# Attention masks of a decoder layer moved to GpSimd and made by saturating arithmetic, with constant operands on ScalarE

## The chip, the core and the metric

The kernel runs on one core of a Trainium2 chip. The core has five engines that run side by side, each with its own queue of instructions: TensorE (PE, matmuls), VectorE (DVE), ScalarE (ACT), GpSimd (POOL) and SyncE (SP), which here issues all DMAs. They wait for each other by semaphores. The metric is the device time of one execution in microseconds.

## What is computed

The kernel is one pre-norm decoder layer over x of shape (8, 128, 128): attention with a hyperbolic distance in 16 heads of 8, then a gated linear attention (mLSTM) over a context in 4 heads, then a mixture of 8 experts. The change is in the first part only:

```python
def _hyperbolic_attention(q, k, v, c, beta, causal=True):
    qn = jnp.sum(q * q, axis=-1)
    kn = jnp.sum(k * k, axis=-1)
    qk = jnp.einsum('bhnd,bhmd->bhnm', q, k)
    diff_sq = jnp.maximum(qn[..., :, None] - 2.0 * qk + kn[..., None, :], 0.0)
    ed = jnp.sqrt(diff_sq + EPS)
    ns = qn[..., :, None] + kn[..., None, :]
    dist_taylor = ed * (1.0 + c * ns * 0.5 + c * c * ns * ns * 0.125)
    dist_asymp = 0.693 + jnp.log(ed + EPS) + c * ns * 0.25
    dist_standard = ed * jnp.sqrt(1.0 + c * ns)
    dist = jnp.where(ed < 0.1, dist_taylor, jnp.where(ed > 2.0, dist_asymp, dist_standard))
    scores = -beta * dist
    if causal:
        scores = jnp.where(tril, scores, -jnp.inf)
    return softmax(scores) @ v
```

Each pair of a query and a key picks one of three formulas for its distance. The kernel works with squares: `e2` is diff_sq, and the two choices are the masks `m_ge` (e2 + 1e-8 >= 0.01, not the Taylor form) and `m_gt` (e2 > 4 - 1e-8, the logarithmic form).

## The kernel before

The attention is cut into 16 units. A unit is a batch and half of its heads, and because of the causal mask only three quarters of the score columns are computed: 768 columns over 128 partitions, in tiles of 128x768. The units pass through a software pipeline written out by hand: every engine has a function `step(s)`, and in step s it works on several units at different stages. All engines run the steps from -1 to 20 in order. Work of units below 0 or above 15 is left out, some steps are in hardware loops, and the last steps have parts of the next stage mixed in (`after`). Nothing reorders instructions within an engine: what is written first is issued first, and waits on semaphores hold everything that is queued behind them on that engine.

One unit u goes this way, with the step in which each engine does it:

- PE: scores P1 (for e2, step u-2) and P2 (for c times ns, `n1` in DVE's code, step u-1), from stacks that SP loads from DRAM. A stack serves two units of a pair of batches; the loads are issued ahead of need, when the scores of the previous holders are done.
- ACT, step u-1: `e2` (Relu, L676), `l1` (Ln of e2, L681), `sqn` (Square, L695) and `wt` (Square, L704), the last two for the Taylor factor.
- DVE, step u-1: `m_ge` (L969), after the wait for e2.
- POOL, step u-1: `m_gt` (L540). It is queued behind the causal additions of unit u-2.
- DVE, step u: `da` (L927, the logarithmic form), then wt is replaced by n1 where m_ge says so (L932, COPY_PREDICATED), then `prod` = (e2 + eps) * wt (L948, SCALAR_TENSOR_TENSOR with both tensors in SBUF).
- ACT, step u: `lp` (Ln of prod, L700) and `dist` (Exp of half of it, L713).
- DVE, step u+1, as the last instruction of the step: dist is replaced by da where m_gt says so (L984, COPY_PREDICATED).
- POOL, step u+1: the causal mask, an addition of 1e30 above the diagonal (L531 and L532, for each of two halves of the unit: four instructions).
- DVE, step u+2: row minima (L941, L943), and their split in three bf16 parts `nmp` (L958 CAST, L973, L976 CAST, L978). PE transposes these, ACT copies them as `shift` (L709), and PE transposes dist with the shift added, 12 pairs of matmuls.
- ACT, step u+3: `pT` (Exp, L686). PE, step u+3: the product with the values. DVE and ACT close a batch in every second pair of steps (L920, L935, L952, L964 and L690).

Tiles named e2, l1, wt, da and prod share one tensor and appear as `dist_mem` in the rows. `P` stands for the PSUM tiles P1, P2 and P3. `cf` is the table of constants: where an ACTIVATE has cf among its inputs, its bias or scale comes as a column of it, read from SBUF. m_ge, m_gt, e2 and da have two buffers each, dist has four. The line numbers in the rows are those of this kernel; matmuls all have L1183, that of a helper.

POOL also clears three tiles after step 5 (L553 to L555), and later splits the expert weights in two parts (L579, L582).

## Time and profile before

| | |
|---|---|
| median of 3 runs | 305.19 us (305.09 to 305.37) |
| span of the profiled execution | 302.1 us |
| PE busy | 224.5 us, 74% |
| DVE busy | 228.1 us, 76% |
| ACT busy | 171.9 us, 57% |
| POOL busy | 109.2 us, 36% |

The span is that of one profiled execution, from its first to its last instruction. The median time also holds what lies around the span. Attention fills the time from about 34 to 150 us; projections and loads stand ahead of it, and the second attention and the experts behind it. A timeline row gives start, duration, engine, line, operation, output<-inputs and shape, and in brackets how long the engine had been idle before it and what it had waited for.

### The profile page before, as it was taken

To read this page: it belongs to the slowest core of one execution; us is meant where nothing else is said; L and a number is where in the kernel's file an instruction comes from. 1 tells how busy PE (TensorE), PEld (TensorE's weight loads), DVE (VectorE), ACT (ScalarE), POOL (GpSimd) and SP (SyncE) were. 2 spreads that over 40 slices of the span, in tenths; PEclk is the share of its full clock that TensorE was granted. 3 is DMA by queue.
4 is the path that set the end of the run, shared out by engine and by line. 5 is a ranking of instruction groups with operands and counts; after the bars stand their busy time and mean duration, and the time that the engine had idled before them with its cause. 6 is when DMAs were issued, how large, how long until landed. Compare 5 with 4: busy or idle time off the path is not lost.

```text
span 302.1 us, 5293 instructions
## 1 busy us (share of the span) xinstructions
PE 224.5 (74%) x1624; PEld 179.0 (59%) x1624; DVE 228.1 (76%) x576; ACT 171.9 (57%) x291; POOL 109.2 (36%) x140
## 2 busy tenths in 40 slices
PE   0867233994778986577766990599896799999994
PEld 0434232773666766465344670487685698888984
DVE  6777799999989999997395349378669976746554
ACT  3599799999499999756511355233432136322320
POOL 5233326777755666652360000000234043424400
PEclk9997655556595579555855796599799599999999
DMA  6208879899404210000000000000000000010001
GB/s 161 69 13 201 171 190 223 195 351 218 116 1 96 48 45 20 0 22 0 1 2 0 0 0 0 2 1 1 2 0 0 0 2 1 2 35 0 0 0 35
DMA packets 38084, 16.80 MB, mean 56 GB/s; under 512 B 19240, under 2 KB 36016, under 8 KB 38064
## 3 DMA queue, kind: packets, MB, share of 16 engines
q1 hardware_dynamic: 38064, 16.56, 21.9%
q8 instruction: 10, 0.16, 0.2%
q14 instruction: 10, 0.08, 0.1%
HBM read 10.39 MB, written 4.98 MB: 51 GB/s over the span
## 4 chain that ended last, share of the span: by engine, by line
PE 44%; DVE 25%; SPq 13%; issue 9%; DMA 4%; ACT 2%; POOL 1%; DVEq 0%; ACTq 0%
PE P L1183 32%; PE PM L1183 7%; PE PO L1183 5%; SPq L369 4%; DVE dist L984 3%; SPq L434 2%; DVE dist_mem L932 2%; SPq L373 2%; DVE m_ge L969 1%; DVE nm L943 1%; DMA n_split<-nsl 1%; SPq L378 1%; DVE dist_mem L948 1%; DMA k_split<-split_mem 1%; SPq L479 1%
## 5 line engine op out<-in xcount | busy, mean ns | idle before, releaser
L782 ACT ACTIVATE dist_mem<-P,gub 128x512 f32<-128x512 f32 x32 | 21.9, 688 | 53.1 <-PE P L1183 51.5
L579 POOL CAST whi<-wgu 128x512 fp32r (+1 forms) x16 | 9.9, 617 | 101.8 <-PE P L1183 101.8
L1112 DVE SCALAR_TENSOR_TENSOR dist_mem<-P,gub,dist_mem 128x512 f32<-128x512 f32 x32 | 23.7, 749 | 22.8 <-ACT dist_mem L782 22.7
L540 POOL TENSOR_SCALAR m_gt<-dist_mem 128x768 uint8<-128x768 f32 x16 | 34.3, 2144 | 6.7 <-issue 4.4
L1183 PE MATMUL P<-cf,dist 128*128 128x128 f32 x96 | 30.0, 398 | 6.6 <-ACT shift L709 6.6
L1183 PE MATMUL P<-xhi,whi 128*128 128x512 f32 x64 | 28.7, 448 | 4.6 <-DVE dist_mem L1112 4.0
L531 POOL TENSOR_TENSOR dist<-dist,cf 128x128 f32<-128x128 f32 x32 | 14.6, 458 | 47.5 <-DVE dist L984 47.5
L1183 PEld LDWEIGHTS P<-cf,dist 128*128 128x128 f32 x96 | 19.5, 203 | 13.4 <-ACT shift L709 9.3
L1183 PE MATMUL P<-shift,cb 128*128 128x128 bf16 x96 | 27.4, 294 | 0.0
L1183 PE MATMUL P<-xlo,whi 128*128 128x512 f32 x64 | 27.2, 425 | 0.0
L1183 PE MATMUL P<-xhi,wlo 128*128 128x512 f32 x64 | 27.2, 425 | 0.0
L1183 PE MATMUL PO<-v_st,pT 128*64 128x9 f32 (+1 forms) x384 | 24.8, 238 | 3.2 <-ACT pT L686 3.1
L1183 PEld LDWEIGHTS PO<-v_st,pT 128*64 128x64 f32 x384 | 23.0, 181 | 5.7 <-ACT pT L686 3.9
L1183 PE MATMUL P<-stn,stq 128*128 128x128 bf16 (+1 forms) x128 | 12.3, 265 | 15.7 <-DVE dist_mem L932 15.7
L582 POOL TENSOR_TENSOR wlo<-wgu,whi 128x512 fp32r<-128x512 f32 x16 | 20.4, 1278 | 2.9 <-POOL whi L579 2.9
L1183 PEld LDWEIGHTS P<-stn,stq 128*128 128x128 bf16 x128 | 9.6, 128 | 19.4 <-issue 19.3
L1183 PE MATMUL P<-stk,stq 128*128 128x128 bf16 (+1 forms) x128 | 11.8, 258 | 8.6 <-DMA stn<-n_split 8.2
L1183 PEld LDWEIGHTS P<-xhi,whi 128*128 128x128 f32 x64 | 13.2, 206 | 7.6 <-issue 5.0
L984 DVE COPY_PREDICATED dist<-m_gt,dist_mem 128x768 f32<-128x768 uint8 x16 | 16.4, 1024 | 0.9
L932 DVE COPY_PREDICATED dist_mem<-m_ge,P 128x768 f32<-128x768 uint8 x16 | 16.3, 1016 | 0.9 <-ACT dist_mem L704 0.9
L927 DVE SCALAR_TENSOR_TENSOR dist_mem<-dist_mem,P 128x768 f32<-128x768 f32 x16 | 15.2, 950 | 2.2 <-ACT sqn L695 1.4
L686 ACT ACTIVATE pT<-P,nbeta 128x768 f32<-128x768 f32 x16 | 14.2, 888 | 3.9 <-PE P L1183 3.8
(221 smaller groups left out, 603.4 us busy)
## 6 DMA issues: line engine op xcount, KB each, us to landing
q_split<-split_mem SPq DMA_DIRECT2D x16, 128.0 KB, 2.8
k_split<-split_mem SPq DMA_DIRECT2D x4, 512.0 KB, 3.6
stq<-q_split SPq DMA_DIRECT2D x16, 128.0 KB
stk<-k_split SPq DMA_DIRECT2D x16, 128.0 KB
v_st<-vab SPq DMA_DIRECT2D x8, 144.0 KB, 2.4
wgu<-gate_w SPq DMA_DIRECT2D x1, 1024.0 KB, 8.7
wgu<-up_w SPq DMA_DIRECT2D x1, 1024.0 KB, 11.3
x_sb<-x SPq DMA_DIRECT2D x2, 256.0 KB, 3.0
```

Of the source, the lines that this page charges most:

```text
L369: sp.dma_start(sq_[k][half[j], :, j, :], q).then_inc(stack_in[k], 16)
L531: pool.tensor_tensor(wideq, wideq, cm, ALU.add)
L540: pool.tensor_scalar(m_gt[:, g.k % 2, :], e2[:, g.k % 2, :], 4.0 - ATT_EPS, None, ALU.is_gt).then_inc(sm["gt_done"], 1)
L579: pool.tensor_copy(hi, w).then_inc(sm["whi_done"], 1)
L582: pool.tensor_tensor(lo, w, hi, ALU.subtract).then_inc(sm["w_ready"], 1)
L686: A(row(pT, t.k % 2), P3[:, :, 0:384], ACT.Exp, scale=nbeta[:, :]).then_inc(sm["pT_done"], 1)
L782: A(sil[:, f, :], P[:, 0, :], ACT.Silu, bias=gub[:, 0, bass.ds(e * FC + f, 1)]).then_inc(sm["sil_done"], 1)
L927: V.scalar_tensor_tensor(row(da, p), row(l1, p), 2.0, n1, ALU.mult, ALU.add).then_inc(sm["da_done"], 1)
L932: V.copy_predicated(row(wt, p), row(m_ge, p), n1).then_inc(sm["sel_done"], 1)
L984: V.copy_predicated(dist[:, far.k % 4, :], m_gt[:, far.k % 2, :], da[:, far.k % 2, :]).then_inc(sm["dist_done"], 1)
L1112: V.scalar_tensor_tensor(hT[:, 2 * slot + f, :], (P1, P2)[f][:, 1, :], gub[:, 1, bass.ds(e * FC + f, 1)], sil[:, f, :], ALU.add, ALU.mult) ...
L1183: return nc.tensor.matmul(out_, lhsT, rhs, start=start, stop=stop, **more)
```

## The change

`m_ge` moves from DVE to POOL, where it is queued between the causal additions and m_gt, with the waits it had (e2_done and sel_done). Both masks are made by addition and multiplication instead of a comparison: e2 minus the limit, times 2 to the 40th, written to uint8. Negative values become 0 and positive ones 255, and a predicated copy takes everything but 0 as true. The limit of m_ge is the largest number that still gives the reference's choice (`below`). The four causal additions become two of twice the size. On ACT four column operands of three instructions (l1's bias, sqn's scale and bias, wt's bias) are constants in the instruction instead.

```diff
+def below(limit, eps):
+    limit, eps = np.float32(limit), np.float32(eps)
+    e = limit
+    while np.float32(e + eps) >= limit:
+        e = np.nextafter(e, np.float32(0))
+    return float(e)
+NEAR_TOP = below(0.01, ATT_EPS)
...
                     wait(pool, "dist_done", g.n(1))
-                    for i in range(2):
-                        row = dist[:, g.k % 4, i * 384:(i + 1) * 384]
...
-                        pool.tensor_tensor(wideq, wideq, cm, ALU.add)
-                        last = pool.tensor_tensor(near, near, cm, ALU.add)
-                    last.then_inc(sm["causal_done"], 1)
+                    rows = dist[:, g.k % 4, :].rearrange("p (i n) -> p i n", i=2)
...
+                    pool.tensor_tensor(wideq, wideq, cm, ALU.add)
+                    pool.tensor_tensor(near, near, cm, ALU.add).then_inc(sm["causal_done"], 1)
                 g = s + 1
                 if g.there():
                     wait(pool, "e2_done", g.n(1))
+                    wait(pool, "sel_done", g.n(-1))
+                    pass_waits(pool)
+                    pool.tensor_scalar(m_ge[:, g.k % 2, :], e2[:, g.k % 2, :], -NEAR_TOP, 2.0 ** 40, ALU.add,
+                                       ALU.mult).then_inc(sm["ge_done"], 1)
                     wait(pool, "dist_done", g.n(-1))
                     pass_waits(pool)
-                    pool.tensor_scalar(m_gt[:, g.k % 2, :], e2[:, g.k % 2, :], 4.0 - ATT_EPS, None,
-                                       ALU.is_gt).then_inc(sm["gt_done"], 1)
+                    pool.tensor_scalar(m_gt[:, g.k % 2, :], e2[:, g.k % 2, :], ATT_EPS - 4.0, 2.0 ** 40, ALU.add,
+                                       ALU.mult).then_inc(sm["gt_done"], 1)
...
-                    A(l1[:, p, :], e2[:, p, :], ACT.Ln, scale=LN_SHIFT, bias=col(K_SEPS)).then_inc(sm["l1_done"], 1)
+                    A(l1[:, p, :], e2[:, p, :], ACT.Ln, scale=LN_SHIFT, bias=LN_SHIFT * ATT_EPS).then_inc(sm["l1_done"], 1)
...
-                    A(row(sqn), ps2, ACT.Square, scale=col(K_R8), bias=col(K_R8)).then_inc(sm["sqn_done"], 1)
+                    A(row(sqn), ps2, ACT.Square, scale=8 ** -0.5, bias=8 ** -0.5).then_inc(sm["sqn_done"], 1)
...
-                    A(wt[:, p, :], sqn[:, :], ACT.Square, bias=col(K_HALF)).then_inc(sm["wt_done"], 1)
+                    A(wt[:, p, :], sqn[:, :], ACT.Square, bias=0.5).then_inc(sm["wt_done"], 1)
...
-                if near.there():
-                    wait(dve, "e2_done", near.n(1))
-                    wait(dve, "sel_done", near.n(-1))
-                    V.tensor_scalar(m_ge[:, near.k % 2, :], e2[:, near.k % 2, :], ATT_EPS, 0.01, ALU.add,
-                                    ALU.is_ge).then_inc(sm["ge_done"], 1)
```

On POOL, one step in the hardware loop stands like this before; dist is the tile with the causal mask added, dist_mem is e2, and the names in brackets are the semaphores waited for:

```order
L531 TENSOR_TENSOR dist<-dist,cf 128x2x64 [waits dist_done]
L532 TENSOR_TENSOR dist<-dist,cf 128x128
L531 TENSOR_TENSOR dist<-dist,cf 128x2x64
L532 TENSOR_TENSOR dist<-dist,cf 128x128
L318 REGISTER_ALU
L540 TENSOR_SCALAR m_gt<-dist_mem 128x768 [waits e2_done,dist_done]
```

and like this now:

```order
L542 TENSOR_TENSOR dist<-dist,cf 128x2x2x64 [waits dist_done]
L543 TENSOR_TENSOR dist<-dist,cf 128x2x128
L330 REGISTER_ALU
L550 TENSOR_SCALAR m_ge<-dist_mem 128x768 [waits e2_done,sel_done]
L554 TENSOR_SCALAR m_gt<-dist_mem 128x768 [waits dist_done]
```

The additions are two instead of four, and m_ge has come in ahead of m_gt.

On DVE, a step of the fill of the pipeline from dist to the split of the minima stands like this before:

```order
L984 COPY_PREDICATED dist<-m_gt,dist_mem 128x768 [waits da_done,ds_done,gt_done]
L927 SCALAR_TENSOR_TENSOR dist_mem<-dist_mem,P 128x768 [waits dist_done,sqn_done,l1_done]
L932 COPY_PREDICATED dist_mem<-m_ge,P 128x768 [waits ge_done,wt_done]
L941 TENSOR_REDUCE nm<-dist 128x2x2 [waits causal_done]
L943 TENSOR_REDUCE nm<-dist 128x2x2
L948 SCALAR_TENSOR_TENSOR dist_mem<-dist_mem 128x768 [waits lp_done,sel_done]
L958 CAST nmp<-nm 128x8 [waits nmT_full,nm0_done]
L969 TENSOR_SCALAR m_ge<-dist_mem 128x768 [waits sel_done,e2_done]
L973 TENSOR_TENSOR nmr<-nm,nmp 128x8 [waits nm1_done]
```

and like this now:

```order
L993 COPY_PREDICATED dist<-m_gt,dist_mem 128x768 [waits da_done,ds_done,gt_done]
L941 SCALAR_TENSOR_TENSOR dist_mem<-dist_mem,P 128x768 [waits dist_done,sqn_done,l1_done]
L946 COPY_PREDICATED dist_mem<-m_ge,P 128x768 [waits ge_done,wt_done]
L955 TENSOR_REDUCE nm<-dist 128x2x2 [waits causal_done]
L957 TENSOR_REDUCE nm<-dist 128x2x2
L962 SCALAR_TENSOR_TENSOR dist_mem<-dist_mem 128x768 [waits lp_done,sel_done]
L972 CAST nmp<-nm 128x8 [waits nmT_full,nm0_done]
L982 TENSOR_TENSOR nmr<-nm,nmp 128x8 [waits nm1_done]
```

The instruction that made m_ge is gone between the cast and the subtraction, and with it its waits; the rest keeps its order.

## Rows read from the trace of the kernel before

**Rows 1.** The page's strip of 40 slices of 7.55 us, busy tenths.

```profile
DVE  6777799999989999997395349378669976746554
ACT  3599799999499999756511355233432136322320
PEclk9997655556595579555855796599799599999999
```

**Rows 2.** Timeline of PE: unit 8's scores.

```profile
76.77 0.80 PE L1183 MATMUL P<-stk,stq 128*128 128x128 bf16 x8 [3.88 <-DMA stn<-n_split]
```

**Rows 3.** Timeline of DVE, one step between two instructions of L984.

```profile
91.67 1.03 DVE L984 COPY_PREDICATED dist<-m_gt,dist_mem 128x768 f32<-128x768 uint8 x1
...
94.52 0.68 DVE L941 TENSOR_REDUCE nm<-dist 128x4 f32<-128x512 f32 x1
...
95.44 0.95 DVE L948 SCALAR_TENSOR_TENSOR dist_mem<-dist_mem 128x768 f32<-128x768 f32 x1
...
96.38 0.73 DVE L969 TENSOR_SCALAR m_ge<-dist_mem 128x768 uint8<-128x768 f32 x1
97.04 0.15 DVE L973 TENSOR_TENSOR nmr<-nm,nmp 128x8 f32<-128x8 f32 x1
97.22 0.17 DVE L976 CAST nmp<-nmr 128x8 bf16<-128x8 f32 x1
...
97.66 1.02 DVE L984 COPY_PREDICATED dist<-m_gt,dist_mem 128x768 f32<-128x768 uint8 x1
```

**Rows 4.** Timeline of POOL in the same step.

```profile
92.78 0.46 POOL L531 TENSOR_TENSOR dist<-dist,cf 128x128 f32<-128x128 f32 x1 [2.18 <-DVE dist L984]
...
94.03 0.46 POOL L532 TENSOR_TENSOR dist<-dist,cf 128x128 f32<-128x128 f32 x1
94.57 2.13 POOL L540 TENSOR_SCALAR m_gt<-dist_mem 128x768 uint8<-128x768 f32 x1
```

**Rows 5.** Groups of DVE from 79 to 135 us: count, busy us, mean ns.

```profile
L969 DVE TENSOR_SCALAR m_ge<-dist_mem 128x768 uint8<-128x768 f32 x8 | 4.7, 589 | 0.0
```

**Rows 6.** Groups of POOL by shape, whole span.

```profile
L540 POOL TENSOR_SCALAR m_gt<-dist_mem 128x768 uint8<-128x768 f32 x16 | 34.3, 2144 | 6.7 <-issue 4.4 <-ACT dist_mem L676 1.1
L582 POOL TENSOR_TENSOR wlo<-wgu,whi 128x512 fp32r<-128x512 f32 x16 | 20.4, 1278 | 2.9 <-POOL whi L579 2.9
L531 POOL TENSOR_TENSOR dist<-dist,cf 128x128 f32<-128x128 f32 x32 | 14.6, 458 | 47.5 <-DVE dist L984 47.5
...
L579 POOL CAST whi<-wgu 128x512 fp32r x14 | 8.6, 614 | 101.8 <-PE P L1183 101.8
...
L567 POOL COPY ctx<-ctx_sb 128x1024 f32<-128x1024 f32 x1 | 1.0, 1036 | 0.0
```

**Rows 7.** Line 948 over the whole span: duration min/median/max in ns.

```profile
L948 DVE SCALAR_TENSOR_TENSOR dist_mem<-dist_mem x16: 942/950/1350, 38.6 to 137.5; 128x768 f32<-128x768 f32 x16
```

**Rows 8.** Timelines of POOL and DVE where line 948 was longest.

```profile
38.34 2.13 POOL L540 TENSOR_SCALAR m_gt<-dist_mem 128x768 uint8<-128x768 f32 x1 [1.12 <-ACT dist_mem L676]
...
38.62 1.35 DVE L948 SCALAR_TENSOR_TENSOR dist_mem<-dist_mem 128x768 f32<-128x768 f32 x1
```

**Rows 9.** Timeline of DVE while POOL clears tiles.

```profile
74.66 3.01 DVE L976 CAST nmp<-nmr 128x8 bf16<-128x8 f32 x1
```

**Rows 10.** Timeline of DVE in the drain.

```profile
149.81 0.69 DVE L941 TENSOR_REDUCE nm<-dist 128x4 f32<-128x512 f32 x1 [1.80 <-POOL dist L532]
```

**Rows 11.** Groups of ACT from 79 to 126 us.

```profile
L713 ACT ACTIVATE dist<-lp 128x768 f32<-128x768 f32 x8 | 6.6, 827 | 0.0
L681 ACT ACTIVATE dist_mem<-dist_mem,cf 128x768 f32<-128x768 f32 x7 | 6.6, 937 | 0.2
```

**Rows 12.** Timeline of PE: the first transposes of two steps.

```profile
98.72 0.48 PE L1183 MATMUL P<-cf,dist 128*128 128x128 f32 x1 [0.36 <-ACT shift L709]
...
104.70 0.48 PE L1183 MATMUL P<-cf,dist 128*128 128x128 f32 x1 [0.36 <-ACT shift L709]
```

**Rows 13.** A stretch of 2 us: busy PE, PEld, DVE, ACT, POOL; PEclk, DMA share, GB/s.

```profile
102.00:104.00 2.00, 2.00 (x28) 1.86 (x26) 1.87 (x8) 2.00 (x3) 0.67 (x1) 0.50 0.39 62
```

More of the change, by code:

```diff
@@ L525, in step @@
                     wait(pool, "dist_done", g.n(1))
-                    for i in range(2):
-                        row = dist[:, g.k % 4, i * 384:(i + 1) * 384]
-                        wideq = row[:, 0:256].rearrange("p (j n) -> p j n", j=2)[:, :, HALF:128]
-                        near = row[:, 256:384].rearrange("p (j n) -> p j n", j=2)
-                        cm = cf[:, C_CM:C_CM + HALF].unsqueeze(1).broadcast_to([128, 2, HALF])
-                        pool.tensor_tensor(wideq, wideq, cm, ALU.add)
-                        last = pool.tensor_tensor(near, near, cm, ALU.add)
-                    last.then_inc(sm["causal_done"], 1)
+                    rows = dist[:, g.k % 4, :].rearrange("p (i n) -> p i n", i=2)
+                    wideq = rows[:, :, 0:256].rearrange("p i (j n) -> p i j n", j=2)[:, :, :, HALF:128]
+                    near = rows[:, :, 256:384].rearrange("p i (j n) -> p i j n", j=2)
+                    cm = cf[:, C_CM:C_CM + HALF].unsqueeze(1).unsqueeze(1).broadcast_to([128, 2, 2, HALF])
+                    pool.tensor_tensor(wideq, wideq, cm, ALU.add)
+                    pool.tensor_tensor(near, near, cm, ALU.add).then_inc(sm["causal_done"], 1)
                 g = s + 1
@@ L910, in step @@
                 n1 = P2[:, :, 0:384]
-                low, far, near = s - 2, s - 1, s + 1
+                low, far = s - 2, s - 1
                 t = s - 4
```

## The prediction

> **What bounds the kernel now.** I read the strip of the span in 40 slices first. VectorE (DVE) is busy 9 tenths or more in slices 6 to 18, with one at 8, and ScalarE (ACT) nearly as much, so in the attention pipeline both look full, and TensorE (PE) runs there mostly at the lower of its two levels [rows 1]. The change touches only this pipeline, roughly 34 to 150 us, and what it shortens must be looked for there; the expert layers behind it have other bounds.
>
> Next I ask where the pipeline is pinned from outside. At 76.77 the score matmuls of unit 8 had waited 3.88 us for the DMA that brings their operands [rows 2]. SyncE's queue before it holds weights and stores and is not waiting for attention work at that point, so whatever the first eight units (0 to 7) gain only lengthens this wait. The gain has to come from units 8 to 15, after 77 us, and from the drain.
>
> There one step of the pipeline takes about 6 us, and the timeline of DVE through one step shows no idle time: `COPY_PREDICATED` into dist at 91.67, and the next one at 97.66, 5.99 us later, with all work laid end to end between [rows 3]. GpSimd (POOL) works 3.9 us of that step and waits 2.18 us for DVE's dist [rows 4]. ACT has next to no idle time either, but the chain of waits of this stretch runs along DVE's instructions. So DVE is what sets the pace, with ACT and, in some steps, PE just under it.
>
> **m_ge leaves DVE.** Eight instructions of line 969 lie behind 77 us, 589 ns on average [rows 5]. The next instruction starts some 0.08 us before such a one ends, so they hold DVE for 4.7 - 8 x 0.08 = 4.1 us. The part of this that is already waiting is included: at 96.38 the instruction took 0.73 us where it takes 0.55 alone, because POOL's m_gt ran until 96.70 [rows 3, 4]. All of it is on the path, as DVE has no gap. Upper end of the gain here: 4.1 us.
>
> **What POOL's instructions cost.** Two facts are needed, and the trace shows neither directly: the price of an add-and-multiply over 768 columns into uint8, and of an addition of 256 columns.
> The additions: 128 columns take 458 ns, 512 columns 1278 ns, both with two inputs [rows 6], so 2.14 ns a column; 256 columns come to 0.73 us, and two of them take 1.4 us where four take 1.7 us. Saved on POOL: 0.3 us a step.
> The masks: the comparison takes 2144 ns for 768 columns, 2.8 ns each. Instructions with one input that don't compare take 614 ns for 512 columns and 1036 ns for 1024, 0.82 ns a column, which gives 0.83 us for 768 [rows 6]. These are the two ends: 0.83 us, if the comparison is what is dear in m_gt, and 2.14 us, if it is the kind of instruction or the uint8 output. I take 0.83 us: the new form is arithmetic on one input, and reading can't be what holds m_gt up, as its input seems to be read within 0.68 us (next part). I keep 2.14 for the rivals.
> The Trainium skill (GPSIMD Engine Reference, section 4.1) says that one-input elementwise work on GpSimd runs at roughly line rate. The row of m_gt speaks against it as a rule for all such work; by the rule the new masks cost what I take, and the row of m_gt taken for the price of every mask leads to the 318 us of the last rival.
>
> **What POOL's instructions do to DVE.** They share a way into SBUF, and this is where the change can pay back its gain. Three things are seen. A `CAST` on DVE that met POOL's memsets took 3.01 us instead of 0.17, through several of them without getting in between [rows 9, 3]. A DVE instruction with two SBUF inputs, line 948, took 1350 ns when it started 0.28 us after an m_gt, 0.40 more than its median of 950 [rows 7, 8]; so m_gt held the reading side until 0.68 us after its start. The same instruction met every later m_gt about 0.9 us after its start and was not held: 15 of 16 are near 950 [rows 7, 3, 4].
> Now lay the new work of a step from the first causal addition at c = 92.78 [rows 4]. The two additions end at c + 1.42, m_ge starts at c + 1.50 (the gap before m_gt in the rows is 0.08), m_gt at about c + 2.38, and ends at c + 3.21. It reads until c + 3.06. Line 948 comes at 95.44, c + 2.66 [rows 3]: it is now held 0.40 us. The small `CAST` comes at c + 3.5 + 0.4, when POOL is done. So such a step gains 0.66 (m_ge with its wait, 96.38 to 97.04) - 0.40 = 0.26 us. In steps that also close a batch, a copy and a reciprocal stand before line 948, 0.2 us, and it is held 0.2 to 0.35 against 0.47 gained. I take 0.2 us a step for the seven steps from unit 8 to unit 14, 1.4 us, and 0.46 in full for the step at 80 to 86 us, where POOL's masks are over before line 948 runs. Together 1.9 us.
> The Trainium skill (SBUF — State Buffer, section Who interferes with whom) says that whoever comes first holds the shared port for its whole instruction. The 15 undisturbed rows of line 948 speak against this for reading. By that rule line 948 would be held until c + 3.21, 0.15 us longer, and the sum would be about 1 us smaller, 304.0.
>
> **The causal additions.** In the steady steps they end before DVE asks for them (94.49 against 94.52), so nothing is gained. In the drain DVE waits for them, 1.80 us up to 149.81, and there the chain passes through them [rows 10]: 0.3 us.
>
> **ScalarE's constants.** An `ACTIVATE` takes 827 ns with constants (L713) and 937 with one column operand (L681) [rows 11]. So a column costs about 0.1 us, and the change drops four a step, 0.40 us. ACT is hidden under DVE in these steps; what it buys is that ACT, which fills the step of 6 us as well, does not become the bound when DVE shrinks. Alone I value it at nothing; without it most of the 1.9 us would be stopped by ACT.
>
> **PE at its lower level.** Between the transposes at 98.72 and at 104.70, 5.98 us, PE idles only 0.36 us for ACT's shift; from 102 to 104 it is busy all the time at a granted clock of 0.50 [rows 12, 13]. Such steps can't shrink below that. There are two of the seven (98 to 107 us); I leave 0.0 to 0.2 us of their 0.4 and take the 0.1 to 0.2 lost here as balanced by ACT's slack, since a fuller PE may be granted 1.00 or not, which no row tells.
>
> **Sum.** 1.9 + 0.3 = 2.2 us off. The profiled execution has a span of 302.1 us and the runs' median is 305.19, 3.1 us more, for what lies around the span; I keep that. 302.1 - 2.2 = 299.9 us of span, 303.0 us of time.
>
> **Rivals.** (a) The forecast: 303.0.
> (b) POOL's fast masks don't hold line 948, since the one held row is from the fill of the pipeline: then all 4.1 us of m_ge, less 0.3 for PE, plus 0.3: 301.1. Against it stands that row.
> (c) The masks cost near 1.0 us. m_gt starts at c + 2.55 and reads until c + 3.23; line 948 is held 0.57 us, and the seven steps give next to nothing. What is left is 0.46 + 0.3 at most: 304.4 to 305.5, within the noise of no change.
> (d) The masks cost 1.2 to 1.6 us. Then m_gt would start at c + 2.75 or later, line 948 comes first, at c + 2.66, and m_gt waits for it until c + 3.6; the `CAST` behind it finds m_gt running until c + 4.8, 1.27 us. Against 0.57 gained that is 0.7 us lost a step, 7 x 0.7 = 4.9: 310.
> (e) The arithmetic costs what the comparison costs, 2.14 us. POOL runs without a gap from c + 1.50 to c + 5.8, the second `CAST` (97.22 less the 0.66 of m_ge, c + 3.78) waits for the end, and dist follows 0.4 us behind it: the step grows from 6.0 to 7.3 us. Seven steps cost 9.1; the six before 76.77 cost 7.8, of which the 3.88 us of DMA wait swallow half, 3.9 left. Total 13: 318. It decides from a mask of about 1.2 us on, with (d) as its mild form. For it: the only mask that the trace has is at 2.14. Against it: every POOL row without a comparison is at 0.8 to 2.1 ns a column.
>
> **How the numbers follow.** (a) 0.43, (b) 0.14, (c) 0.13, (d) 0.12, (e) 0.18. Faster by over 0.2%, 0.6 us, which is about what a measurement here can tell: (a) and (b), 0.57. Within it: (c), 0.13. Slower: (d) and (e), 0.30. The range runs from 300.5, a little under (b), to 311, past (d), and leaves out (e). The likeliest case by itself spans 302 to 304.3.
>
> **What the profile of the changed kernel would show.** Right: m_ge and m_gt on POOL near 0.85 us each; line 962 (line 948 before) between 1.1 and 1.4 us instead of 0.95; the distance from dist to dist on DVE near 5.7 us between 86 and 118 us; ACT's l1 and wt near 0.83 us, with idle time ahead of some; the wait of unit 8's scores for the DMA longer than 3.88 us and ending still near 76.8. Wrong: masks over 1.1 us, the small casts at over 0.5 us in each step, or POOL without idle time. The forecast also falls if the DMA before 76.77 is in truth released by attention work, for then the early steps would count as well.

## The result and the profile after

| | before | changed |
|---|---|---|
| median, both on one chip | 305.28 us (4 runs) | 313.33 us (312.90 to 314.52, 4 runs) |
| ratio of the two, 95% interval | | 1.0247 [1.0211, 1.0283] |
| span of the profiled execution | 302.1 us | 311.1 us |
| mean granted clock of PE | 0.77 | 0.74 |

The kernel is 8 us slower. The forecast was 303.0 us, in a range up to 311: wrong in sign, and the time lies outside the range.

Where the 9.0 us of span come from can be read from DVE's selects into dist, one a step. The one at 77.93 us before stands at 79.47 now, 1.5 us later; seven steps on, 122.54 has become 131.62. So 7.5 us arise in seven steps, 1.08 us in each; from there to the end of the program the distance stays between 8.8 and 9.8. The page's strip, of the same rows as [rows 1] and of POOL:

```profile
DVE  6767767777877777799579166657778976756554
ACT  3589898778777887782741256125423134522320
POOL 5123344336533333333182000000224033424310
PEclk9997655555555555555675699569989799999999
```

DVE is no longer full where it was at 9, ACT has room too, and POOL is busy for 96.7 us where it was for 109.2. PE is granted half its clock in all of slices 6 to 19. No engine is busy throughout, so they wait for each other. The groups of the whole span say for what. After the bar come busy us, mean ns of one, and the idle time ahead of them with its releasers:

```profile
L946 DVE COPY_PREDICATED dist_mem<-m_ge,P 128x768 f32<-128x768 uint8 x16 | 16.2, 1013 | 17.2 <-POOL m_ge L550 16.6
...
L554 POOL TENSOR_SCALAR m_gt<-dist_mem 128x768 uint8<-128x768 f32 x16 | 13.9, 867 | 1.3
L550 POOL TENSOR_SCALAR m_ge<-dist_mem 128x768 uint8<-128x768 f32 x16 | 13.3, 830 | 5.0 <-issue 3.6 <-ACT dist_mem L690 1.4
L542 POOL TENSOR_TENSOR dist<-dist,cf 128x256 f32<-128x256 f32 x16 | 11.7, 729 | 68.7 <-DVE dist L993 68.7
```

DVE waited 16.6 us for m_ge, a wait that did not exist before. And POOL, which makes m_ge, waited 68.7 us for DVE's dist. Two engines that wait for each other are a loop, and one step of the timelines of DVE and POOL (the step of [rows 3, 4]) shows it closed:

```profile
94.82 1.02 DVE L993 COPY_PREDICATED dist<-m_gt,dist_mem 128x768 f32<-128x768 uint8 x1
95.88 0.95 DVE L941 SCALAR_TENSOR_TENSOR dist_mem<-dist_mem,P 128x768 f32<-128x768 f32 x1
98.32 1.01 DVE L946 COPY_PREDICATED dist_mem<-m_ge,P 128x768 f32<-128x768 uint8 x1 [1.49 <-POOL m_ge L550]
...
100.14 0.95 DVE L962 SCALAR_TENSOR_TENSOR dist_mem<-dist_mem 128x768 f32<-128x768 f32 x1
...
101.93 1.02 DVE L993 COPY_PREDICATED dist<-m_gt,dist_mem 128x768 f32<-128x768 uint8 x1
```

```profile
95.93 0.73 POOL L542 TENSOR_TENSOR dist<-dist,cf 128x256 f32<-128x256 f32 x1 [4.55 <-DVE dist L993]
96.61 0.72 POOL L543 TENSOR_TENSOR dist<-dist,cf 128x256 f32<-128x256 f32 x1
97.30 0.83 POOL L550 TENSOR_SCALAR m_ge<-dist_mem 128x768 uint8<-128x768 f32 x1
98.21 0.83 POOL L554 TENSOR_SCALAR m_gt<-dist_mem 128x768 uint8<-128x768 f32 x1
103.04 0.73 POOL L542 TENSOR_TENSOR dist<-dist,cf 128x256 f32<-128x256 f32 x1 [4.00 <-DVE dist L993]
```

DVE's last instruction of a step is the select (94.82). POOL's additions wait for it (95.93), m_ge is queued behind them (97.30 to 98.13), and the second full-width instruction of DVE's very next step needs that m_ge (98.32). From there DVE has 3.61 us of work to the next select. The four pieces, 1.11 + 1.37 + 1.02 + 3.61, are the step of 7.11 us, where it was 5.99 [rows 3]. e2, the input of m_ge, had long been there: ACT had made it by 89.94.

### The profile page after: what moved, and what is told of

Its sections match the earlier page's. It is cut to its first block, busy times and chain, and to the rows that moved or that the text cites. A ratio compares the mean times of both kernels' runs of the same rounds, so it can differ in the third digit from the quotient of the medians.

```text
span 311.1 us, 5263 instructions
## 1 busy us (share of the span) xinstructions
PE 232.9 (75%) x1624; PEld 186.7 (60%) x1624; DVE 221.5 (71%) x560; ACT 169.0 (54%) x291; POOL 96.7 (31%) x124
## 4 chain that ended last, share of the span: by engine, by line
PE 36%; issue 23%; DVE 19%; POOL 11%; ACT 5%; DMA 3%; SPq 1%; POOLq 0%; DVEq 0%; ACTq 0%
PE P L1192 26%; PE PM L1192 5%; PE PO L1192 5%; POOL m_gt L554 3%; POOL m_ge L550 3%; POOL dist L543 3%; DMA k_split<-split_mem 1%; DMA stn<-n_split 1%; DVE xn L887 1%; DVE dist L993 1%; DMA x_sb<-x 1%; DVE ctx_sb L1135 1%; DVE w_mem L1023 1%; ACT dist_mem L796 1%; DVE dist_mem L962 1%
## 5 line engine op out<-in xcount | busy, mean ns | idle before, releaser
L1192 PE MATMUL P<-cf,dist 128*128 128x128 f32 x96 | 32.3, 421 | 6.2 <-ACT shift L723 6.2
L542 POOL TENSOR_TENSOR dist<-dist,cf 128x256 f32<-128x256 f32 x16 | 11.7, 729 | 68.7 <-DVE dist L993 68.7
L1192 PE MATMUL PO<-v_st,pT 128*64 128x9 f32 (+1 forms) x384 | 29.9, 260 | 3.0 <-ACT pT L700 3.0
L1192 PEld LDWEIGHTS PO<-v_st,pT 128*64 128x64 f32 x384 | 28.1, 216 | 6.1 <-ACT pT L700 3.8
L1192 PE MATMUL P<-xhi,whi 128*128 128x512 f32 x64 | 27.6, 431 | 4.7 <-DVE dist_mem L1121 4.0
L1192 PE MATMUL P<-shift,cb 128*128 128x128 bf16 x96 | 29.3, 308 | 0.0
L1192 PEld LDWEIGHTS P<-cf,dist 128*128 128x128 f32 x96 | 20.8, 217 | 13.8 <-ACT shift L723 9.1
L946 DVE COPY_PREDICATED dist_mem<-m_ge,P 128x768 f32<-128x768 uint8 x16 | 16.2, 1013 | 17.2 <-POOL m_ge L550 16.6
L1192 PE MATMUL P<-xhi,wlo 128*128 128x512 f32 x64 | 26.3, 411 | 0.0
L709 ACT ACTIVATE sqn<-P 128x768 f32<-128x768 f32 x16 | 12.9, 807 | 11.4 <-PE P L1192 11.4
L1192 PE MATMUL P<-stk,stq 128*128 128x128 bf16 (+1 forms) x128 | 12.9, 272 | 5.4 <-DMA stn<-n_split 5.0
```

Of the source, the lines that this page charges most:

```text
L542: pool.tensor_tensor(wideq, wideq, cm, ALU.add)
L709: A(row(sqn), ps2, ACT.Square, scale=8 ** -0.5, bias=8 ** -0.5).then_inc(sm["sqn_done"], 1)
L946: V.copy_predicated(row(wt, p), row(m_ge, p), n1).then_inc(sm["sel_done"], 1)
L1192: return nc.tensor.matmul(out_, lhsT, rhs, start=start, stop=stop, **more)
```

## Experiments

The kernel before ran beside them, with medians of 304.65 to 305.29 us, and the ratio is to its runs beside the kernel in question. "Step" is the mean of six steps in the pipeline's steady part behind unit 8, from select into dist to select into dist on DVE (from the seventh to the thirteenth of the 16 selects), in the one profiled execution of each kernel.

| kernel | median us | ratio, 95% interval | step us |
|---|---|---|---|
| before | 305.3 | | 6.16 |
| changed | 313.33 | 1.0247 [1.0211, 1.0283] | 7.41 |
| ge_stays | 305.28 | 0.9993 [0.9960, 1.0025] | 6.17 |
| gt_arith | 304.86 | 0.9987 [0.9958, 1.0017] | 6.27 |
| ge_move_alone | 318.84 | 1.0449 [1.0398, 1.0499] | 7.69 |
| no_causal | 300.70 | 0.9855 [0.9810, 0.9900] | 6.24 |
| ge_compare | 340.01 | 1.1151 [1.1095, 1.1207] | 9.47 |
| ge_first | 303.63 | 0.9960 [0.9936, 0.9985] | 6.02 |
| ge_first_cols | 303.51 | 0.9949 [0.9921, 0.9977] | 6.03 |
| ge_first_swap | 304.55 | 0.9999 [0.9970, 1.0028] | 6.15 |
| ge_late | 304.48 | 0.9984 [0.9960, 1.0008] | 5.86 |
| ge_late_cols | 303.96 | 0.9961 [0.9936, 0.9987] | 5.94 |
| ge_after_prod | 305.31 | 1.0008 [0.9980, 1.0035] | 6.36 |
| before_loads | 303.80 | 0.9953 [0.9923, 0.9983] | 6.30 |
| after_loads | 313.70 | 1.0267 [1.0224, 1.0311] | 7.42 |
| ge_first_loads | 299.39 | 0.9819 [0.9787, 0.9852] | 6.19 |
| ge_late_loads | 299.56 | 0.9814 [0.9776, 0.9851] | 5.85 |

### Which part of the change is slow

ge_stays is the changed kernel with m_ge back on DVE:

```diff
-                    wait(pool, "sel_done", g.n(-1))
-                    pass_waits(pool)
-                    pool.tensor_scalar(m_ge[...], e2[...], -NEAR_TOP, 2.0 ** 40, ALU.add, ALU.mult)
...
+                if near.there():
+                    wait(dve, "e2_done", near.n(1))
+                    wait(dve, "sel_done", near.n(-1))
+                    V.tensor_scalar(m_ge[...], e2[...], ATT_EPS, 0.01, ALU.add, ALU.is_ge)
```

> All of the change except the move: m_ge is made by VectorE, by comparison, at its old place; m_gt by arithmetic, two causal additions and ScalarE's constants stay. Theory A (the loss is the wait of VectorE's select for m_ge, which stands on GpSimd behind the causal additions, which stand behind VectorE's own last instruction of the step): that wait of 1.4 us a step is gone, and the kernel is at 305.3 or up to 1.5 us below it, since GpSimd's shorter work no longer stretches m_ge and the casts. Theory B (the loss is in the port that VectorE and GpSimd share, through faster GpSimd instructions): the fast m_gt and the large additions are still there, and at least 2 of the 8 us stay, 307 or more.

ge_move_alone is the kernel before with nothing but m_ge moved (both diffs of the change that concern it), and gt_arith the kernel before with only m_gt made by arithmetic.

> Only m_ge moves to GpSimd, by arithmetic, behind the causal additions; m_gt stays a comparison, the causal additions stay four, ScalarE keeps its column operands. Theory A: the step is dist's select 1.0, additions 1.65, m_ge 0.83 and the rest of VectorE's step, 7.3 us instead of 7.0 in the changed kernel, so 13 steps cost 0.27 us more each: about 316 us. Theory B: the second mask still takes 2.13 us and the shared port is held as in the kernel before, so the time is between the two kernels, 305 to 313.

> Only m_gt is made by addition and multiplication; nothing else is changed. Theory A: m_gt takes 0.83 instead of 2.14 us, nobody waits for it; it no longer stretches m_ge and the cast on VectorE (0.1 to 0.2 us in some four steps behind 77 us): 0.3 to 0.8 us faster than before, 304.5 to 305.0. Theory B: the fast instruction holds line 948 and the time grows by 1 us or more.

ge_stays is the kernel before again, in time and in step. ge_move_alone carries the whole loss and more, 318.84 us where about 316 were expected. DVE waits there 1.6 to 1.8 us for m_ge, and the step is 0.28 us longer than in the changed kernel, as four additions (1.67 us) stand in the loop instead of two (1.37). gt_arith, with a mask that is 1.3 us shorter on POOL, changes nothing measurable. So it is the move of m_ge that costs, and the additions in two instructions only make it cheaper.

### Is it the place in the queue

no_causal leaves the additions nearly out (four single columns of them are left, so the causal mask is not applied) and leaves m_ge where the change puts it:

```diff
-                    pool.tensor_tensor(wideq, wideq, cm, ALU.add)
-                    pool.tensor_tensor(near, near, cm, ALU.add).then_inc(sm["causal_done"], 1)
+                    pool.tensor_tensor(near[:, :, :, 0:1], near[:, :, :, 0:1], cm[:, :, :, 0:1],
+                                       ALU.add).then_inc(sm["causal_done"], 1)
```

> The changed kernel with the causal additions cut down to one column (256 blocks of 64 columns become 4 single columns), so the causal mask is left out. Theory A: the path from dist's select to the next m_ge loses some 1.2 us, the wait of 1.39 us shrinks to 0.1 to 0.2, and the step goes from 7.0 to 5.8 us: 303 to 305 us. Theory B: the wait for m_ge is not what sets the step; the time stays above 310.

ge_compare lengthens another link of the loop, m_ge itself:

```diff
-                    pool.tensor_scalar(m_ge[...], e2[...], -NEAR_TOP, 2.0 ** 40, ALU.add, ALU.mult)
+                    pool.tensor_scalar(m_ge[...], e2[...], ATT_EPS, 0.01, ALU.add, ALU.is_ge)
```

> The changed kernel with m_ge on POOL by comparison (add, is_ge) in the place that the change gives it. A comparison of this size takes 2.14 us on POOL. Theory A (m_ge is on a loop dist, additions, m_ge, n1, dist): each microsecond on the mask is a microsecond on the step, 1.3 us more in each, 7.3 becomes 8.6; eight steps behind 77 us cost 10.4, and the steps ahead of it another 5 to 8, as the slack before unit 8's loads is used up: 327 to 332. Theory B (only POOL's interference counts): m_gt and m_ge overlap more of DVE's work, 2 to 5 us in all, 315 to 318.

ge_first leaves all links as long as they are and takes m_ge out of the loop, by writing it ahead of the additions:

```diff
             def step(s):
+                g = s + 1
+                if g.there():
+                    wait(pool, "e2_done", g.n(1))
+                    wait(pool, "sel_done", g.n(-1))
+                    pass_waits(pool)
+                    pool.tensor_scalar(m_ge[...], e2[...], -NEAR_TOP, 2.0 ** 40, ALU.add, ALU.mult)
                 g = s - 1
                 if g.there():
                     wait(pool, "dist_done", g.n(1))
...
                     pool.tensor_tensor(near, near, cm, ALU.add).then_inc(sm["causal_done"], 1)
                 g = s + 1
                 if g.there():
-                    wait(pool, "e2_done", g.n(1))
-                    wait(pool, "sel_done", g.n(-1))
-                    pass_waits(pool)
-                    pool.tensor_scalar(m_ge[...], e2[...], -NEAR_TOP, 2.0 ** 40, ALU.add, ALU.mult)
                     wait(pool, "dist_done", g.n(-1))
```

> The changed kernel with one thing moved: on POOL m_ge of unit s+1 stands ahead of the causal additions of unit s-1, not behind them. POOL waits about 2 us in each step for DVE's dist, and e2 of unit s+1 should be ready in that time, so m_ge (0.83 us) fits in there and costs POOL nothing. Theory A (the loss is m_ge's place in POOL's queue, behind a wait for dist): line 946's wait for m_ge goes from 1.39 to near 0, a step from 7.3 to 5.7-6.0 us, the time 301 to 303.5; m_gt then starts 0.83 us earlier and may hold the product (two SBUF tensors) by up to 0.4 us. Theory B (the loss is that POOL has more to do and gets in DVE's way, or that the arithmetic masks are dear): the amount of work on POOL is the same, so the time stays at 310 or more.

In no_causal DVE's wait for m_ge is down to 0.23 to 0.34 us behind unit 8, the mean step is back at 6.24, and the time is 300.70, below the 303 to 305 expected. Part of that is not the loop: in the drain DVE waits twice for the additions, 1.5 us each in the changed kernel and 0.3 here, 2.4 us in all. (The profiled execution of no_causal took 304.59 us, with unit 8's operands late, at 79.06; the other four took 300.64 to 301.05. They have no profile, so it is not shown that these operands made the difference.) In ge_compare the timeline of POOL shows a dearer mask than I had expected, and that of DVE the wait behind it:

```profile
103.42 2.77 POOL L550 TENSOR_SCALAR m_ge<-dist_mem 128x768 uint8<-128x768 f32 x1
```

```profile
106.38 1.01 DVE L946 COPY_PREDICATED dist_mem<-m_ge,P 128x768 f32<-128x768 uint8 x1 [3.46 <-POOL m_ge L550]
```

2.77 us, not 2.14: it adds and compares where m_gt only compares. The mask is 1.94 us longer than the arithmetic one, DVE's wait in this step grows by 2.07 (3.46 against 1.39, at 90.66 in the changed kernel), and the mean step by 2.06. Expected were 327 to 332 us from a mask of 2.14; it came to 340. The slope is the point: what is put on m_ge is added to the step nearly one for one, and theory B's 315 to 318 is out. ge_first does the same work on the same engines as the changed kernel, in another order, and is 9.7 us faster (9.1 if each is first set against its own runs of before). DVE no longer waits for m_ge at all. With these three the cause of the 8 us is settled: m_ge's place behind a wait for dist.

### Why it is no faster where the loop is gone

ge_first is what the forecast had described: m_ge off DVE at no cost in waiting. It was to give 303.0 us, and gave 303.63, 1.0 us less than before in the runs beside it, where the forecast took off 2.2. But the agreement hides that a step like that of [rows 3] is 5.99 us here as there, not the 5.7 of the prediction; the mean of six is 6.02 against 6.16. DVE and POOL of ge_first in such a step:

```profile
93.01 0.83 POOL L557 TENSOR_SCALAR m_gt<-dist_mem 128x768 uint8<-128x768 f32 x1
93.92 0.83 POOL L540 TENSOR_SCALAR m_ge<-dist_mem 128x768 uint8<-128x768 f32 x1
```

```profile
90.40 1.02 DVE L996 COPY_PREDICATED dist<-m_gt,dist_mem 128x768 f32<-128x768 uint8 x1
...
94.14 1.40 DVE L965 SCALAR_TENSOR_TENSOR dist_mem<-dist_mem 128x768 f32<-128x768 f32 x1
95.47 0.16 DVE L975 CAST nmp<-nm 128x8 bf16<-128x8 f32 x1
95.66 0.17 DVE L985 TENSOR_TENSOR nmr<-nm,nmp 128x8 f32<-128x8 f32 x1
95.87 0.17 DVE L988 CAST nmp<-nmr 128x8 bf16<-128x8 f32 x1
...
96.39 1.02 DVE L996 COPY_PREDICATED dist<-m_gt,dist_mem 128x768 f32<-128x768 uint8 x1 [0.15 <-issue]
```

The product (line 965, line 948 of before) takes 1.40 us instead of 0.95. Over the whole span (min/median/max in ns) it took longer in most steps, where before the median was 950 [rows 7]:

```profile
L965 DVE SCALAR_TENSOR_TENSOR dist_mem<-dist_mem x16: 937/1289/1404, 38.5 to 135.6; 128x768 f32<-128x768 f32 x16
```

That was so in 11 of the 16. The one at 94.14 ends at 95.54; 0.95 before that is 94.59, which is 0.67 us after m_ge started on POOL. That is the holding of [rows 8] with its 0.68 us: POOL delays the product until that long after its own start. From product to select it was 95.44 to 97.66 before, 2.22 us [rows 3], and is 94.14 to 96.39 here, 2.25. Leaving out m_ge saved 0.54 us between the first small `CAST` and the subtraction (0.73 before, 0.19 now), the holding took 0.46, and the select came 0.08 later behind the last small instruction.

Does the pace follow if the holding is removed? ge_late is ge_first with one wait more:

```diff
                     wait(pool, "sel_done", g.n(-1))
+                    if (s - 2).there():
+                        wait(pool, "nm_done", (s - 2).n(1))
```

> As ge_first, with one wait more: on POOL m_ge of unit s+1, ahead of the causal additions, also waits for the last part of the minima of unit s-2 (nm_done), so it starts as DVE begins its last instruction of the step, the select into dist, 1.1 us before the additions. With m_ge right after m_gt, as in ge_first, line 965 (the product, two SBUF inputs) takes 1.2 to 1.4 us instead of 0.95, and the step stays at 5.97 to 6.1 us. Theory H (the two masks back to back hold the product, and that has eaten the gain of taking m_ge off DVE): the product is back at 0.95 us, a step is 0.3 to 0.45 us shorter (5.6 to 5.7, then bounded by ACT, whose instructions fill 5.74), and the time is 1.5 to 3 us below ge_first: 300.5 to 302. Rival R (ACT or PE bounds the step at 6.0 whatever DVE does): the product is short again, DVE idles 0.3 to 0.4 us a step, and the time stays within 0.7 us of ge_first. Rival S: m_ge now holds the select into dist, which reads two tensors and a mask: that takes 1.4 us instead of 1.02, and nothing is gained.

ge_after_prod has `if s.there(): wait(pool, "prod_done", s.n(1))` in that place:

> As ge_late, but m_ge waits for the product of unit s (prod_done) instead. It then runs beside DVE's small casts, the split of the minima. If a small cast must wait for the whole of POOL's instruction that runs (as where it took 3.01 us beside POOL's memsets), one cast takes up to 0.9 us, the step gets 0.3 to 0.5 us longer than in ge_late, and the time is 1 to 3 us above ge_late: 302.5 to 304.5. If only POOL's reading holds it (0.68 us from its start), the first cast is the one held and loses 0.5 us. If casts are not held: as ge_late.

In both the product is back at 0.95 us behind the fill, so the diagnosis holds for the product. The times did not follow: 304.48 where 300.5 to 302 was expected, and 305.31 where 302.5 to 304.5 was. m_ge meets something else each time. In ge_late, on POOL and DVE:

```profile
98.55 1.55 POOL L542 TENSOR_SCALAR m_ge<-dist_mem 128x768 uint8<-128x768 f32 x1 [1.97 <-DVE nmp L992]
100.07 0.73 POOL L552 TENSOR_TENSOR dist<-dist,cf 128x256 f32<-128x256 f32 x1
```

```profile
98.42 1.02 DVE L998 COPY_PREDICATED dist<-m_gt,dist_mem 128x768 f32<-128x768 uint8 x1
```

Rival S had it the wrong way round: the select is not held, it holds. It started 0.13 us earlier, and m_ge takes 1.55 us instead of 0.83. The additions behind it end late, and the minima come up to 0.3 us later for it (at 95.70, 1.17 us after the start of the copy into wt; 0.90 in ge_first). The step is still shorter, 5.81, and 5.86 in the mean: 0.30 less than before, 0.16 less than ge_first. In ge_after_prod m_ge ran from 97.83 to 98.66 beside the small instructions:

```profile
97.47 0.16 DVE L977 CAST nmp<-nm 128x8 bf16<-128x8 f32 x1
97.66 0.17 DVE L987 TENSOR_TENSOR nmr<-nm,nmp 128x8 f32<-128x8 f32 x1
97.86 0.82 DVE L990 CAST nmp<-nmr 128x8 bf16<-128x8 f32 x1
```

The cast ended only at 98.68, so it was held by the whole of POOL's instruction, not by 0.68 us of it; the mean step is 6.36. In these rows there are two sorts of holding: a `CAST` is held by all of POOL's instruction, a two-input product by its first 0.68 us. The Trainium skill (SBUF — State Buffer, section SBUF: two separate sides) has one rule, the whole instruction, for both; the row of the cast agrees, the 1.40 of the product does not (by the rule it would have ended at 95.70, not 95.54).

ge_first_swap, ge_first with the product ahead of the minima on DVE, was the other way to move the product, and was no better, 304.55; the product was still held, in 13 of 16 rows:

> As ge_first, but on DVE the product stands ahead of the row minima of unit s-2, so that ACT's logarithm and exponential of it start 0.9 us earlier and the product meets another stretch of POOL's work. If DVE is full, nothing is gained, and the transposes of PE, which wait for the minima, come 0.95 us later: 0 to 2 us slower than ge_first. If the chain product, lp, dist, select is what is late (DVE idle ahead of the last select): 0.5 to 2 us faster than ge_first.

### Are ScalarE's constants worth anything

ge_first_cols and ge_late_cols are ge_first and ge_late with the column operands of before (`bias=col(K_SEPS)` and the other three).

> As ge_first, m_ge ahead of the causal additions, but with ScalarE's four column operands of before instead of constants. It tells what the constants are worth once DVE has become shorter. If ACT, which has 0.4 us more work a step, is next in line: 1 to 2.5 us slower than ge_first. If ACT is covered: within 0.5 us of it.

> As ge_late, but with ScalarE's four column operands of before. In ge_first with columns ACT had 6.0 us of work in a step of 5.99 and idled 0.0, with constants it idled 0.28 us. If DVE's step gets shorter in ge_late, ACT with columns cannot follow: steps stay at 5.97 to 6.0 us and the time is 1 to 2.5 us above ge_late. If ge_late's step does not get shorter: the two agree within 0.7 us.

Constants and columns agree in both pairs, 303.63 and 303.51, 304.48 and 303.96. ACT of ge_first from 79 to 126 us, first with constants, then with columns:

```profile
L698 ACT ACTIVATE dist_mem<-dist_mem 128x768 f32<-128x768 f32 x8 | 6.7, 844 | 0.3
...
L717 ACT ACTIVATE lp<-dist_mem 128x768 f32<-128x768 f32 x7 | 5.9, 844 | 2.0 <-DVE dist_mem L965 2.0
...
L712 ACT ACTIVATE sqn<-P 128x768 f32<-128x768 f32 x7 | 5.7, 810 | 0.1
```

```profile
L712 ACT ACTIVATE sqn<-P,cf 128x768 f32<-128x768 f32 x7 | 6.9, 987 | 0.0
...
L698 ACT ACTIVATE dist_mem<-dist_mem,cf 128x768 f32<-128x768 f32 x7 | 6.5, 936 | 0.2
...
L717 ACT ACTIVATE lp<-dist_mem 128x768 f32<-128x768 f32 x7 | 5.9, 844 | 0.7 <-DVE dist_mem L965 0.4
```

A column costs 0.09 us (0.11 between the two instructions of [rows 11]), two of them 0.18. What the constants save turns up as ACT's wait for the product, 2.0 us instead of 0.4. ge_late_cols was expected to be stopped by ACT at 5.97 us a step and to be 1 to 2.5 us slower than ge_late. Its steps are 5.94, 0.08 above ge_late's, and its time is 0.5 us below: no cost of the columns is shown.

### Where ge_late's shorter steps went

Its steps are 0.30 us shorter than before's in the mean, and its time is not. Its profile shows PE's wait for unit 8's operands, the one of [rows 2]:

```profile
78.71 0.80 PE L1197 MATMUL P<-stk,stq 128*128 128x128 bf16 x8 [6.67 <-DMA stn<-n_split]
```

Over the profiled executions of ten kernels (all with the weights in their old place whose steps are near before's) these operands came at 76.4 to 79.1 us, after waits of up to 7.1 us: what an early unit gains ends there, and the landing's own scatter, 2.7 us, is more than ge_late's steps gain behind it. That is not all. Counted from its landing, the profile of ge_late is 2.5 us ahead of that of before at the thirteenth select (43.25 us against 45.77), and only 0.6 at the end (224.7 against 225.3): the rest goes in the drain, and ge_late_loads below shows part of how.

The last four kernels issue the loads of the expert weights (three of the five big loads that stand ahead of unit 8's in SyncE's queue) behind the attention's loads instead:

```diff
             sp.dma_start(ctxT[:, :], ctx_t).then_inc(sm["ctx_in"], 16)
-            sp.dma_start(wgu[:, :, 0, :], ...)
-            sp.dma_start(wgu[:, :, 1, :], ...)
-            sp.dma_start(wd[:, :, :], ...)
             with sp.Fori(2, NP) as bp:
                 for k in range(2):
                     next_stack(bp, k)
                     next_values(bp - 1, k)
+            sp.dma_start(wgu[:, :, 0, :], ...)
+            sp.dma_start(wgu[:, :, 1, :], ...)
+            sp.dma_start(wd[:, :, :], ...)
```

> The kernel before, with the three loads of the expert weights (3 MB and more, issued by SyncE at 58 to 63 us) issued behind the last loads of attention operands instead of ahead of unit 8's. If those weights are what unit 8's scores wait for (3.88 us in the kernel before), that wait goes to near 0 and the time falls by about 3.9 us, to 301.4. If the wait is the queue's own slowness or the stacks' scattered small packets, it stays and the time is the same, 305.

> The changed kernel with the expert weights issued late. Its unit 8 waited only 1.15 us, since the loop over m_ge had already taken the time: theory A expects 1.15 us less, 312, and 10 to 11 us between it and before_loads (8 us between the two without this edit), because nothing of the 1.0 to 1.4 us a step is now swallowed by the DMA wait ahead of unit 8.

> m_ge ahead of the causal additions, and the expert weights issued late. ge_first waited 4.31 us for unit 8's operands: 299.3 if that goes. Its steps of 5.97 to 6.1 us are as long as before's where a product of 1.2 to 1.4 us eats the gain, so it should lie 0.5 to 2 us under before_loads.

> m_ge timed to start with DVE's select into dist, and the expert weights issued late. If the landing of unit 8's operands hid the gain of the shorter steps: 14 steps of 5.8 instead of 6.0 us, 2.5 us less than before_loads plus its 0.5 to 1.5 us elsewhere, 297.5 to 299.5, and 0.5 to 2 us under ge_first_loads. If PE and ACT set the pace once unit 8 is no longer late: steps of 6.0 us here too and within 0.5 us of ge_first_loads.

The wait is gone from all four profiles: the weights were its cause. after_loads gains nothing, where the 1.15 us of its wait were expected, and is 9.9 us behind before_loads. before_loads gains 1.3 us, not 3.9. Its DVE, right behind the time that was gained, runs into POOL's clearing of tiles:

```profile
73.81 3.60 DVE L969 TENSOR_SCALAR m_ge<-dist_mem 128x768 uint8<-128x768 f32 x1
```

The clearing held a `CAST` for 3.01 us in the kernel before [rows 9]; there the unit-8 wait lay behind it and hid it. Later the moved weights land (103 to 117 us, busy PE, PEld, DVE, ACT, POOL, PEclk, DMA share, GB/s; before_loads first, then before):

```profile
103.00:117.00 14.00, 13.07 (x115) 10.89 (x113) 13.10 (x28) 12.48 (x21) 7.65 (x10) 0.50 0.89 262
```

```profile
103.00:117.00 14.00, 11.55 (x131) 9.47 (x129) 13.47 (x32) 13.64 (x22) 7.65 (x10) 0.71 0.22 50
```

PE is granted 0.50 (1.2 GHz) there instead of 0.71 and is busy 13.07 of 14 us; two steps take 6.68 us. The DMA traffic alone doesn't make the clock: in the same stretch ge_late_loads had a DMA share of 0.77 and was granted 0.74, and PE had 0.50 in the whole pipeline of the changed kernel, with a share of 0.19. Whether it has a part in it isn't settled.

ge_first_loads and ge_late_loads keep the gain: 299.4 and 299.6 us, 1.8% and 1.9% faster than before. That is the 299.3 expected of the first, and just above the range of the second, which was to be 0.5 to 2 us under the first and is not. ge_late_loads runs its six steps in 35.1 us where ge_first_loads needs 37.2, and is 2.8 us ahead at 116 us. In the drain, where DVE also prepares the next attention (norms and gate weights), it loses 1.1 of them in two steps. In the first, m_ge and the additions of POOL meet those small DVE instructions. ge_late_loads has

```profile
117.26 0.80 DVE L1005 COPY wg<-wg_raw 128x36 f32<-128x36 f32 x1
118.10 0.67 DVE L1006 TENSOR_TENSOR wg<-wg_raw 128x36 f32<-128x36 f32 x1
```

where the first takes 0.18 us in ge_first_loads; here it ended at 118.06, with m_ge, which ran to 118.02. The next step loses as much, 0.53, and the one behind it 1.1; their causes, and that of the rest, are open.

## Why the prediction was wrong

**The step that failed** is in the part "What POOL's instructions do to DVE". It set m_ge at c + 1.50, c being the first causal addition, and that was right to 0.13 us: 97.30 with c = 95.93. But the text went on to m_gt and to what both do to DVE's instructions by sharing the way into SBUF, and never asked who waits for m_ge and when. It put this wait at nothing without a reason, and took the 0.66 us of m_ge off the path as if its result were free. The trace of before had the answer, in a row that [rows 3] leave out:

```profile
93.60 1.02 DVE L932 COPY_PREDICATED dist_mem<-m_ge,P 128x768 f32<-128x768 uint8 x1
```

DVE replaced dist at 91.67 and needed m_ge 1.93 us later, at c + 0.82 with c = 92.78. m_ge would end at c + 2.33. That is 1.5 us late, in each step, less the 0.54 to 0.66 that DVE saves, so 0.85 to 0.97 us a step. What the runs showed in place of nothing: a wait of 1.37 to 1.49 us in each steady step, and 1.08 us more a step. Before, DVE made m_ge of a unit one step ahead, with hardly more than e2 to wait for. On POOL it keeps its unit and its step, but is queued behind an instruction that waits for the last work of DVE's step, and so can't be ahead any more. The order rows of the change show the two lines one under the other, `[waits dist_done]` and m_ge below it; the edit adds no wait to m_ge, its neighbour's wait is inherited.

**The rivals.** (d) and (e) end on the slower side, at 310 and 318, but both by masks dearer than the 0.83 us that was measured. None of the five had this mechanism, and that 310 and 318 lie on either side of 313.3 is chance.

**Masks.** Forecast 0.83 us, measured 0.83 and 0.87. The comparison was what was dear, [rows 6].

**Additions.** 0.73 each, as forecast (0.729, 0.727). They are worth 0.28 us a step once they stand in a loop (ge_move_alone), and nothing in the steady steps of ge_stays. The forecast took 0.3 us for one wait in the drain; there are two, and each went from 1.80 to 1.52 us.

**Holding.** The size was right: the product takes 1.35 to 1.40 us where it meets a mask that has just started. In the changed kernel it happened only in the fill, at 37.83 us, because the loop moved the product to 100.14, 1.93 us behind m_gt. Where m_ge is early (ge_first) it did eat the gain, and more than forecast: the step compared above gained 0.0, not 0.26, as DVE saved 0.54 and not 0.66, the holding was 0.46 and not 0.40, and the select came a little later; the mean of six steps gained 0.14. The prediction's reading that line 948 met every later m_gt about 0.9 us after its start is too simple: it was 0.87 to 1.07 us in 10 rows, 1.40 and 1.66 in two, and three met no m_gt.

**DMA ahead of unit 8.** The forecast was that early gains are lost there, and the waits agree: 4.31 us in ge_first, 6.67 in ge_late. That the wait would grow was wrong for the changed kernel: the early steps were longer too, and took it from 3.88 down to 1.15 us:

```profile
77.95 0.80 PE L1192 MATMUL P<-stk,stq 128*128 128x128 bf16 x8 [1.15 <-DMA stn<-n_split]
```

Where this slack is gone, the change costs 9.9 us, the distance of after_loads from before_loads.

**Constants.** Priced rightly (0.09 us each), and valued at nothing alone, which is right. That most of the gain would be stopped by ACT without them was wrong: with columns nothing was lost that could be measured (303.51 against 303.63).

**PE.** The granted clock went to 0.50 in the whole pipeline. PE was busy 26.52 of 32 us from 86 to 118 us, so it was not the bound even so. ge_first, with the same work in another order, was granted 0.70 from 79 to 107 us; what made the clock fall in the changed kernel wasn't tested.

## What to carry to other kernels

When an instruction moves to another engine, write down two times from the old trace before any price: when the instruction ahead of it in its new queue is released, and when its result is first needed. If the release comes from the end of the consumer's own step, the two queues form a loop, and every link of it is paid in every step, whatever share of time the engines are busy. The place in the queue was worth 9 to 10 us here, while a mask outside the loop that became 1.3 us shorter (m_gt in gt_arith) changed nothing measurable.

A gain ahead of a fixed event (here operands behind the expert weights in one DMA queue) is no gain; look for what pins the time first, and take that away together with the change. That is what made 299.4 us of 305.1.

## What was not expected of the hardware

- On POOL, addition and multiplication of 128x768 from fp32 to uint8 takes 0.83 us, one comparison 2.14 us, and addition with comparison 2.77 us.
- DVE's `COPY_PREDICATED` with all inputs in SBUF holds POOL: m_ge took 1.45 to 1.57 us when it started 0.12 to 0.22 us after one (ge_late). With its data in PSUM it held nothing: in ge_late m_gt started at 69.95, 0.18 us after the copy of line 951, and took 0.83.
- A small `CAST` (128x8) on DVE is held by POOL until POOL's instruction ends (0.82 instead of 0.17 us); a product of two SBUF tensors only until 0.67 to 0.69 us after POOL's start, whether POOL's instruction lasts 0.83 us (ge_first), 2.13 (before) or 2.77 (ge_compare, at 39.17).
